# Moving two GpSimd residual additions ahead of the mixing weights, and one convolution tap behind the first scores

## The chip, the core and the metric

The kernel runs on one core of one Trainium2 chip. The metric is the device time of one execution in microseconds; the time before is the median of three runs. The profile is of a separate execution.

## What is computed

One transformer-like convolution layer over x of shape (128, 384, 14, 14), N = 196 pixels, 8 heads, key depth 32, value depth 128:

```
g  = groupnorm(x, 32 groups)
q, k, v4 = 1x1 convolutions of g (256, 256, 1024 channels), scaled and shifted
vl = depthwise 3x3 convolution of v4, scaled and shifted
attn = q k^T * scale + bias;  attn = th1w attn + th1b (mix over heads)
attn = softmax(attn);         attn = th2w attn + th2b (mix over heads)
o = relu(attn v + vl)
out = x + 1x1 convolution of o to 384 channels
```

## The kernel before

The 128 images are taken two at a time: 64 steps `t`, the first and the last written out and the 62 between them in a hardware loop. The work of each engine is an order written by hand; engines meet through semaphores, and what an engine has in its program runs strictly in that order.

In one step **TensorE** runs: 12 tiles of q, k and v (line 289 into `psA`), projection tiles 0 and 1 of the step before, 14 logit groups `n` (line 289 into `psL` and `psM`, two query rows of pixels each), projection tile 2, 14 mixing groups (line 396), and 8 groups of attention times value, `u` = 0 to 7 (line 418). Group u = 2 writes the bank that u = 0 used, so it waits until VectorE has added u = 0 into `acc` (semaphore `s_add`).

**VectorE** runs per step 64 taps of the depthwise convolution (line 687, `convs`), 16 low halves `q_lo` (709), two transposes (717), 28 scores (742, two for each logit group; each is an instruction that adds the bias and takes the maximum, and a short read of the accumulator), two reciprocals (752, 757), and then 8 additions (778) and 8 low halves `o_lo` (771). The taps come from one list: channel pair by channel pair, 16 taps each, and `convs(count)` takes the next `count`. Tap 0 of a channel reads `vpad` and `acc`, both in SBUF (shown as `psC<-vpad,par,shared`); taps 1 to 6 read `vpad` and PSUM (`psC<-vpad,par,psC`); tap 7 writes `acc` (`shared<-vpad,par,psC`). Whatever is left of the 64 runs behind the second reciprocal, in `convs(64)`, ahead of the first addition.

**GpSimd** (POOL) runs per step: two `k_lo` (841), four small instructions and the normalisation of the next pair (804), the mixing weights of image 0 and of image 1 (826, four instructions each: 448, 448, 448 and 224 columns), the three residual additions (815, `residual(t, m)`, one for each projection tile), and `x_lo` (809). Mixing weights of image 0 wait for the first reciprocal, those of image 1 for the second; a residual addition waits for ScalarE's eviction of its projection tile and, the first of them, for the loaded x (`s_res`). The names `acc` and `res` are parts of `shared`.

**SyncE** stores the result when all three residual additions are done, waits for that store, and then loads the next `res`.

Of the kernel before, what the change touches and what calls it, by code (L numbers as in the profile page):

```python
# [12 lines left out]
CT = DIM // P  # L13
# [30 lines left out]
def build(nc, A, out):  # L44
# [4 lines left out]
    with ExitStack() as ctx:  # L49
# [9 lines left out]
        def sem(name):  # L59
            return ctx.enter_context(nc.semaphore(name))  # L60
# [91 lines left out]
        s_x, s_res = sem("s_x"), sem("s_res")  # L152
# [54 lines left out]
        def wait_alone(eng, semaphore, value):  # L207

            eng.wait_ge(semaphore, value)
            eng.nop(nofuse=True)  # L210
# [400 lines left out]
        def _(dve):  # L611
# [78 lines left out]
            def step(t, first, last):  # L690
                todo = iter([(c, n) for c in range(0, VT, 2) for n in range(16)])

                def convs(count):
                    for _ in range(count):
                        nxt = next(todo, None)
                        if nxt:
                            conv(t, first, *nxt)

                if not first:
                    dve.wait_ge(s_olo, 8 * t)  # L700
                    dve.wait_ge(s_av_mm, 8 * t)
                low_half = iter([(kt, g) for kt in range(QT) for g in range(NH)])

                def mixed_low(count):
                    for _ in range(count):
                        kt, g = next(low_half)
                        dve.wait_ge(s_qhi, 16 * t + 8 * kt + g + 1)
                        dst, src = mixed(kt, g)
                        nc.vector.scalar_tensor_tensor(q_lo[dst], src, th1[:, kt, g:g + 1], q_hi[dst].bitcast(f32),  # L709
                                                       MUL, SUB).then_inc(s_qlo, 1)  # L710

                def turn(half):
                    c0 = half * (VT // 2)
                    dve.wait_ge(s_v_sb, VT * t + c0 + VT // 2)
                    src = vpad[:, c0:c0 + VT // 2, PITCH + 1:PITCH + 1 + 2 * PITCH * PITCH].rearrange(
                        "p c (i n) -> p c i n", i=2)[:, :, :, 0:BLOCKS * BLK]
                    nc.vector.transpose(turned[:, :, :, c0:c0 + VT // 2, :].rearrange("p i b c n -> p c (i b) n"),  # L717
                                        src).then_inc(s_turned, 1)

                if first:  # L720
                    dve.wait_ge(s_bias, 1)
                    dve.wait_ge(s_ones, 1)
                convs(6)
                for _ in range(8):
                    mixed_low(1)
                    convs(1)
                if not first:
                    dve.wait_ge(s_mix_mm, 14 * t)
                turn(0)
                convs(2)  # L730
                mixed_low(3)
                turn(1)
                mixed_low(5)
                convs(6)
                for n in range(RES):
                    if n == TURNED_ROW // 2:
                        dve.wait_ge(s_vt_out, OUTS * (t + 1))
                    wait_alone(dve, s_logit_mm, 14 * t + n + 1)
                    for r in (2 * n, 2 * n + 1):
                        img, b = divmod(r, RES)  # L740
                        at_ = (RES - 1 - b) * RES
                        nc.vector.tensor_tensor_reduce(  # L742
                            out=keys(img, b),
                            in0=logit_bank(n)[:, (r % 2) * PIX:(r % 2 + 1) * PIX].rearrange("p (r w) -> p r w", w=RES),
                            in1=bias[:, at_:at_ + PIX].rearrange("p (r w) -> p r w", w=RES),
                            scale=-1.0, scalar=3.4028234e38, op0=ADD, op1=ALU.min,
                            accum_out=nmax[:, img, b:b + 1]).then_inc(s_score, 1)
                    if n == 10:
                        dve.wait_ge(s_exp, 28 * t + 14)
                        if not first:  # L750
                            dve.wait_ge(s_mixw, 8 * t)
                        nc.vector.reciprocal(rinv[:, 0, :], rowsum[:, 0, :]).then_inc(s_rinv, 1)  # L752
                    if n:
                        convs(1)
                convs(3)
                dve.wait_ge(s_exp, 28 * t + 28)
                nc.vector.reciprocal(rinv[:, 1, :], rowsum[:, 1, :]).then_inc(s_rinv, 1)
                convs(3)
                convs(64)

                if first:
                    dve.wait_ge(s_wplo, 1)
                else:
                    dve.wait_ge(s_proj_mm, 3 * t)

                def low(u):
                    img, n = divmod(u, 4)
                    dve.wait_ge(s_relu, 8 * t + u + 1)
                    a = acc[:, 2 * n:2 * n + 2, img * IMG:img * IMG + PIX]
                    sl = (slice(None), slice(2 * n, 2 * n + 2), slice(img * PIX, (img + 1) * PIX))  # L770
                    nc.vector.scalar_tensor_tensor(o_lo[sl], a, 0.0, o_hi[sl].bitcast(f32), ALU.max, SUB).then_inc(s_olo, 1)

                for u in range(8):
                    img, n = divmod(u, 4)
                    dve.wait_ge(s_conv, 64 * t + 16 * (n + 1))
                    dve.wait_ge(s_av_mm, 8 * t + u + 1)
                    a = acc[:, 2 * n:2 * n + 2, img * IMG:img * IMG + PIX]
                    nc.vector.tensor_tensor(a, psA[:, n % 2, 0:COLS].rearrange("p (c n) -> p c n", c=2), a,  # L778
                                            ADD).then_inc(s_add, 1)
                    if u:  # L780
                        low(u - 1)
                low(7)
# [4 lines left out]
        def _(pool):  # L787
# [13 lines left out]
            def normalise(p):  # L801
                wait_alone(pool, s_rstd, p + 1)
                for i in range(2):
                    nc.gpsimd.tensor_scalar(xs[:, i, :, :], xs[:, i, :, :], gs[:, i, 0:1], rstd[:, i:i + 1],
                                            SUB, MUL).then_inc(s_xn, 1)
# [6 lines left out]
            def residual(t, m):  # L812

                wait_alone(pool, s_pout, 3 * (t - 1) + m + 1)
                nc.gpsimd.tensor_tensor(res[:, :, m, :], proj[:, m, :].rearrange("p (i n) -> p i n", i=2),
                                        res[:, :, m, :], ADD).then_inc(s_out, 1)

            def mixing_weights(t, first, img):

                if not first:  # L820
                    pool.wait_ge(s_mix_mm, 14 * (t - 1) + 7 * (img + 1))
                pool.wait_ge(s_rinv, 2 * t + img + 1)
                for b0 in range(0, RES, 4):
                    nb = min(4, RES - b0)
                    k2 = kron2[:, :, :].rearrange("p g i -> p (g i)").unsqueeze(1).broadcast_to([HP, nb, HP])
                    nc.gpsimd.tensor_tensor(mixw[0:HP, img, b0:b0 + nb, :], k2,  # L826
                                            rinv[:, img, b0:b0 + nb].unsqueeze(2).broadcast_to([HP, nb, HP]),
                                            MUL).then_inc(s_mixw, 1)
# [9 lines left out]
            def step(t, first, last):  # L838
                for kt in range(QT):
                    wait_alone(pool, s_khi, 2 * t + kt + 1)  # L840
                    nc.gpsimd.tensor_tensor(k_lo[:, kt, :], k[:, kt, :], k_hi[:, kt, :].bitcast(f32),  # L841
                                            SUB).then_inc(s_klo, 1)
                if not last:
                    reciprocal_deviation(t + 1)
                    normalise(t + 1)
                mixing_weights(t, first, 0)
                mixing_weights(t, first, 1)
                if first:
                    pool.wait_ge(s_wphi, 1)
                    nc.gpsimd.tensor_tensor(wp_lo[:, :, :], stage_p, wp_hi[:, :, :].bitcast(f32), SUB).then_inc(s_wplo, 1)  # L850
                if not first:
                    pool.wait_ge(s_res, 16 * t)
                    for m in range(CT):
                        residual(t, m)
                if not last:
                    pool.wait_ge(s_v_mm, VT * (t + 1))
                    if not first:
                        pool.wait_ge(s_out, 3 * t)
                    x_low(t + 1)
# [54 lines left out]
```

## Time and profile before

| | |
|---|---|
| median of 3 runs | 4620.49 us (4615.77 to 4624.45) |
| profiled execution, its own time | 4580.5 us |
| its span | 4578.4 us |
| PE busy | 4526.2 us (99%) |
| DVE busy | 4213.5 us (92%) |
| ACT busy | 3571.4 us (78%) |
| POOL busy | 1437.7 us (31%) |

The profiled execution is 39.99 us shorter than the median of the timed runs. Matmul records overlap one another, so a busy PE says only that something was under way. "Chain" below is the chain of work that ended last. A row of a timeline gives start, length, engine, line, operation, output<-inputs and shapes; the idle time ahead of it stands in brackets with what ended it. A record is longer than the step from it to the next one by about 0.1 us where instructions follow each other directly.

### The profile page before, as it was taken

How to read it: one execution, taken by the hardware profiler on the slowest of the kernel's cores; microseconds unless marked ns; L12 is line 12 of the kernel's file. 1: busy time of each engine (PE TensorE's matmuls, PEld its weight loads, DVE VectorE, ACT ScalarE, POOL GpSimd, SP SyncE). 2: the span in 40 equal slices, each digit the busy share in tenths (PEclk: the TensorE clock that was granted, in tenths of full speed). 3: DMA queues.
4: the chain of work that ended last, by engine and by line, in shares of the span. 5: the costliest groups of instructions: out<-in, count | busy, mean ns of one | idle time of the engine just before them, and what ended most of it. 6: DMA issues, size and time to landing. Idle time of an engine off the chain costs nothing.

```text
span 4578.4 us, 108323 instructions
## 1 busy us (share of the span) xinstructions
PE 4526.2 (99%) x33666; PEld 4504.7 (98%) x33666; DVE 4213.5 (92%) x10012; ACT 3571.4 (78%) x8508; POOL 1437.7 (31%) x1285
## 2 busy tenths in 40 slices
PE   6999999999999999999999999999999999999999
PEld 6999999999999999999999999999999999999999
DVE  8999999999999999999999999999999999999998
ACT  5877878778787787787877877878778777787786
POOL 3323233233332332323323323233233332332322
PEclk8999999999999999999999999999999999999999
DMA  3223222222232222322222223222222232222322
GB/s 91 77 67 96 64 80 81 75 84 67 77 96 64 80 80 69 91 64 80 86 74 80 76 68 96 64 80 85 73 82 69 75 96 64 80 80 71 89 64 75
DMA packets 210732, 356.04 MB, mean 78 GB/s; under 512 B 15842, under 2 KB 132690, under 8 KB 210644
## 3 DMA queue, kind: packets, MB, share of 16 engines
q1 hardware_dynamic: 210708, 355.74, 26.7%
q8 instruction: 13, 0.21, 0.0%
q14 instruction: 11, 0.09, 0.0%
HBM read 199.70 MB, written 155.98 MB: 78 GB/s over the span
## 4 chain that ended last, share of the span: by engine, by line
PE 95%; DVE 4%; issue 1%; DMA 0%; DVEq 0%; ACT 0%; POOL 0%; POOLq 0%
PE psA L289 44%; PE psA L418 13%; PE psL L289 13%; PE psM L289 10%; PE psM L396 8%; PE psL L396 6%; DVE psC L687 1%; DVE shared L687 1%; DVE shared L778 1%; DVE probs L742 0%; PE psA L302 0%; DVE xs L664 0%; DVE q_lo L709 0%; DMA xs<-in_x 0%; DVE probs L717 0%
## 5 line engine op out<-in xcount | busy, mean ns | idle before, releaser
L687 DVE SCALAR_TENSOR_TENSOR psC<-vpad,par,psC 128x406 f32<-128x406 f32 x3072 | 1804.4, 641 | 0.0
L576 ACT ACTIVATE probs<-probs,nmax 112x196 f32<-112x196 f32 x1792 | 803.1, 450 | 120.8 <-DVE nmax L742 112.6
L289 PE MATMUL psA<-x_hi,w_lo 128*128 128x392 f32 x2304 | 794.6, 345 | 15.5 <-DVE x_lo L668 15.5
L289 PE MATMUL psA<-x_hi,w_hi 128*128 128x392 f32 x2304 | 785.9, 341 | 0.0
L289 PE MATMUL psA<-x_lo,w_hi 128*128 128x392 f32 x2304 | 784.9, 341 | 0.0
L418 PE MATMUL psA<-qa,shared 105*128 105x196 f32 x4096 | 710.1, 332 | 16.2 <-DVE shared L778 8.2
L418 PEld LDWEIGHTS psA<-qa,shared 105*128 105x128 f32 x4096 | 677.7, 191 | 35.3 <-DVE shared L778 35.2
L841 POOL TENSOR_TENSOR k_lo<-qk,k_hi 128x392 fp32r<-128x392 f32 x128 | 160.1, 1250 | 1669.3 <-ACT k_hi L482 1669.3
L709 DVE SCALAR_TENSOR_TENSOR q_lo<-qk,th,q_hi 128x392 fp32r<-128x392 f32 x1024 | 618.8, 633 | 0.0
L453 ACT ACTIVATE o_hi<-shared 128x392 fp32r<-128x392 f32 x512 | 271.7, 531 | 426.4 <-DVE shared L778 426.3
L478 ACT ACTIVATE q_hi<-qk,th 128x392 fp32r<-128x392 f32 x1024 | 594.8, 618 | 2.1
L826 POOL TENSOR_TENSOR mixw<-kron,rinv 112x448 f32<-112x448 f32 (+1 forms) x512 | 462.4, 934 | 268.8 <-DVE rinv L752 156.2
L289 PE MATMUL psL<-k_hi,q_lo 128*112 128x196 f32 x2048 | 534.2, 261 | 6.6 <-DVE q_lo L709 6.6
L289 PE MATMUL psL<-k_lo,q_hi 128*112 128x196 f32 x2048 | 536.2, 262 | 0.0
L289 PE MATMUL psL<-k_hi,q_hi 128*112 128x196 f32 x2048 | 535.9, 262 | 0.0
L289 PE MATMUL psA<-o_hi,wp_lo 128*128 128x392 f32 x1536 | 526.5, 343 | 0.0
L289 PE MATMUL psA<-o_lo,wp_hi 128*128 128x392 f32 x1536 | 523.0, 341 | 0.0
L289 PE MATMUL psA<-o_hi,wp_hi 128*128 128x392 f32 x1536 | 521.0, 339 | 0.0
L687 DVE SCALAR_TENSOR_TENSOR psC<-vpad,par,shared 128x406 f32<-128x406 f32 x512 | 331.9, 671 | 142.8 <-ACT shared L448 142.7
L502 ACT ACTIVATE vpad<-psA,par 128x392 f32<-128x392 f32 x512 | 349.6, 683 | 144.8 <-PE psA L289 138.2
L289 PEld LDWEIGHTS psA<-x_hi,w_lo 128*128 128x128 f32 x2304 | 434.3, 188 | 15.9 <-issue 15.9
L396 PE MATMUL psM<-mixw,probs 113*105 113x112 f32 x4096 | 436.0, 260 | 0.0
(83 smaller groups left out, 10804.0 us busy)
## 6 DMA issues: line engine op xcount, KB each, us to landing
by_key<-probs SPq DMA_DIRECT2D x512, 224.0 KB, 3.6
qa<-by_key SPq DMA_DIRECT2D x128, 448.0 KB, 4.3
qk<-by_key SPq DMA_DIRECT2D x128, 448.0 KB, 7.0
xs<-in_x SPq DMA_DIRECT2D x64, 588.0 KB, 5.1
shared<-in_x SPq DMA_DIRECT2D x64, 588.0 KB, 3.8
out<-shared SPq DMA_DIRECT2D x63, 588.0 KB, 3.0
qa<-in_wqkv SPq DMA_DIRECT2D x3, 768.0 KB, 8.1
stage_wp<-in_wp SPq DMA_DIRECT2D x1, 1536.0 KB, 10.5
```

Source lines behind the costliest of these rows:

```text
L289: last = nc.tensor.matmul(dst, w, r, start=(begin and n == 0), stop=(end and n == 2))
L396: mm = nc.tensor.matmul(bank[:, jc, :, b, :], probs[0:HP + 1, img, 2 * n + b, jc * HALF:(jc + 1) * HALF], mixw[0:HP + 1, img, 2 * n + b, : ...
L418: mm = nc.tensor.matmul(psA[:, u % 2, e * PIX:(e + 1) * PIX], vt[0:HALF, img, jc, g * D:(g + 1) * D], attn[:, img, jc, g, :], start=(jc == ...
L453: nc.scalar.activation(o_hi[:, 2 * n:2 * n + 2, img * PIX:(img + 1) * PIX], acc[:, 2 * n:2 * n + 2, img * IMG:img * IMG + PIX], ACT.Relu). ...
L478: nc.scalar.activation(q_hi[dst], src, ACT.Copy, scale=th1[:, kt, g:g + 1]).then_inc(s_qhi, 1)
L502: nc.scalar.activation(dst[:, :, 0:RES, 0:RES], psA[:, m % 2, 0:COLS].rearrange("p (i r w) -> p i r w", i=2, w=RES), ACT.Identity, bias=qk ...
L576: nc.scalar.activation(row, row, ACT.Exp, bias=nmax[:, img, b:b + 1], scale=-1.0, accum_out=rowsum[:, img, b:b + 1]).then_inc(s_exp, 1)
L687: nc.vector.scalar_tensor_tensor(a if tap == 7 else sums, src, taps[:, c, TAPS[tap]:TAPS[tap] + 1], a if tap == 0 else sums, MUL, ADD).the ...
L709: nc.vector.scalar_tensor_tensor(q_lo[dst], src, th1[:, kt, g:g + 1], q_hi[dst].bitcast(f32), MUL, SUB).then_inc(s_qlo, 1)
L778: nc.vector.tensor_tensor(a, psA[:, n % 2, 0:COLS].rearrange("p (c n) -> p c n", c=2), a, ADD).then_inc(s_add, 1)
L826: nc.gpsimd.tensor_tensor(mixw[0:HP, img, b0:b0 + nb, :], k2, rinv[:, img, b0:b0 + nb].unsqueeze(2).broadcast_to([HP, nb, HP]), MUL).then_ ...
L841: nc.gpsimd.tensor_tensor(k_lo[:, kt, :], k[:, kt, :], k_hi[:, kt, :].bitcast(f32), SUB).then_inc(s_klo, 1)
```

## The change

On VectorE, the logit loop takes one tap behind the scores of group n = 0 too; so far it took one behind each of n = 1 to 13. On GpSimd, the residual additions of projection tiles 0 and 1 (with the wait for `s_res`) go ahead of the mixing weights; tile 2 stays behind them.

```diff
@@ VectorE, in the loop over the 14 logit groups
                         nc.vector.reciprocal(rinv[:, 0, :], rowsum[:, 0, :]).then_inc(s_rinv, 1)
-                    if n:
-                        convs(1)
+                    convs(1)
                 convs(3)
@@ GpSimd, in step
                     reciprocal_deviation(t + 1)
                     normalise(t + 1)
+                if not first:
+                    pool.wait_ge(s_res, 16 * t)
+                    residual(t, 0)
+                    residual(t, 1)
                 mixing_weights(t, first, 0)
                 mixing_weights(t, first, 1)
...
                 if not first:
-                    pool.wait_ge(s_res, 16 * t)
-                    for m in range(CT):
-                        residual(t, m)
+                    residual(t, 2)
```

VectorE's order at the first scores, before: two logit groups are scored in a row, then the first tap follows.

```order
50 L742 ISA probs,nmax<-psL,bias 112x14x14
51 L742 ISA nmax 112x1
52 L742 ISA probs,nmax<-psL,bias 112x14x14
53 L742 ISA nmax 112x1
54 L742 ISA probs,nmax<-psL,bias 112x14x14
55 L742 ISA nmax 112x1
56 L687 SCALAR_TENSOR_TENSOR psC<-vpad,par,psC 128x406
```

The same place now:

```order
50 L742 ISA probs,nmax<-psL,bias 112x14x14
51 L742 ISA nmax 112x1
52 L687 SCALAR_TENSOR_TENSOR psC<-vpad,par,psC 128x406
53 L742 ISA probs,nmax<-psL,bias 112x14x14
54 L742 ISA nmax 112x1
55 L742 ISA probs,nmax<-psL,bias 112x14x14
56 L742 ISA nmax 112x1
57 L687 SCALAR_TENSOR_TENSOR psC<-vpad,par,psC 128x406
```

A tap stands ahead of the scores of group 1. VectorE's order from the first reciprocal on, groups 10 to 12, before:

```order
101 L752 RECIPROCAL rinv<-rowsum 112x14
102 L687 SCALAR_TENSOR_TENSOR shared<-vpad,par,psC 128x406
103 L742 ISA probs,nmax<-psM,bias 112x14x14
104 L742 ISA nmax 112x1
105 L742 ISA probs,nmax<-psM,bias 112x14x14
106 L742 ISA nmax 112x1
107 L687 SCALAR_TENSOR_TENSOR psC<-vpad,par,shared 128x406
108 L742 ISA probs,nmax<-psL,bias 112x14x14
```

and now:

```order
102 L752 RECIPROCAL rinv<-rowsum 112x14
103 L687 SCALAR_TENSOR_TENSOR psC<-vpad,par,shared 128x406
104 L742 ISA probs,nmax<-psM,bias 112x14x14
105 L742 ISA nmax 112x1
106 L742 ISA probs,nmax<-psM,bias 112x14x14
107 L742 ISA nmax 112x1
108 L687 SCALAR_TENSOR_TENSOR psC<-vpad,par,shared 128x406
109 L742 ISA probs,nmax<-psL,bias 112x14x14
```

Every tap stands one group sooner: the two taps 0, with both inputs in SBUF, stand behind the scores of groups 10 and 11 instead of 11 and 12. GpSimd's order in the loop, as the difference:

```order
+L814 TENSOR_TENSOR shared<-proj,shared 128x2x196
+L820 ISA
+L825 TENSOR_TENSOR mixw<-kron,rinv 112x448 x3
+L825 TENSOR_TENSOR mixw<-kron,rinv 112x224
+L820 REGISTER_ALU
+L825 TENSOR_TENSOR mixw<-kron,rinv 112x448 x3
+L825 TENSOR_TENSOR mixw<-kron,rinv 112x224
 L209 REGISTER_ALU
-L815 TENSOR_TENSOR shared<-proj,shared 128x2x196
-L856 ISA
-L858 REGISTER_ALU
-L809 TENSOR_TENSOR x_lo<-xs,x_hi 128x1176
+L814 TENSOR_TENSOR shared<-proj,shared 128x2x196
```

Two residual additions come ahead of the eight mixing-weight instructions, and one is left behind them.

## Rows read from the trace of the kernel before

**Rows 1.** The page's chain that ended last, by engine

```profile
PE 95%; DVE 4%; issue 1%; DMA 0%; DVEq 0%; ACT 0%; POOL 0%; POOLq 0%
```

**Rows 2.** Chain in order of time, one step: start, length, what

```profile
2008.41 8.23 PE psA L418 x48
...
2046.84 1.18 PE psM L289 x12
...
2065.53 1.54 PE psM L396 x16
...
2076.27 1.36 PE psA L418 x8
...
2077.90 0.64 DVE shared L687
...
2079.07 8.23 PE psA L418 x48
```

**Rows 3.** Timeline of VectorE behind the last scores

```profile
2061.94 2.28 DVE L687 SCALAR_TENSOR_TENSOR psC<-vpad,par,psC 128x406 f32<-128x406 f32 x4
2064.13 0.23 DVE L757 RECIPROCAL rinv<-rowsum 112x14 f32<-112x14 f32 x1
```

**Rows 4.** Timeline of VectorE at the first scores

```profile
2046.38 0.08 DVE L742 DVE_READ_ACCUMULATOR2_ANT nmax<- 112x1 f32 x1
2046.99 0.36 DVE L742 CUSTOM_DVE_ANT_0 probs<-psL,bias 112x196 f32<-112x196 f32 x1 [0.53 <-PE psL L289]
```

**Rows 5.** Waits of the whole span: total, times, longest

```profile
DVE probs L742 <- PE psL L289: 34.4, 64, 1.2
```

**Rows 6.** Timeline of VectorE, second step

```profile
140.28 0.64 DVE L687 SCALAR_TENSOR_TENSOR psC<-vpad,par,psC 128x406 f32<-128x406 f32 x1
140.82 0.36 DVE L742 CUSTOM_DVE_ANT_0 probs<-psM,bias 112x196 f32<-112x196 f32 x1
```

**Rows 7.** Timeline of VectorE, logit groups 10 to 12

```profile
2058.55 0.56 DVE L687 SCALAR_TENSOR_TENSOR shared<-vpad,par,psC 128x406 f32<-128x406 f32 x1
2059.02 0.36 DVE L742 CUSTOM_DVE_ANT_0 probs<-psM,bias 112x196 f32<-112x196 f32 x1
...
2059.58 0.65 DVE L687 SCALAR_TENSOR_TENSOR psC<-vpad,par,shared 128x406 f32<-128x406 f32 x1
2060.19 0.37 DVE L742 CUSTOM_DVE_ANT_0 probs<-psL,bias 112x196 f32<-112x196 f32 x1
...
2060.76 0.70 DVE L687 SCALAR_TENSOR_TENSOR psC<-vpad,par,shared 128x406 f32<-128x406 f32 x1
```

**Rows 8.** Timeline of GpSimd, same step (rows may overlap)

```profile
2052.06 4.66 POOL L804 TENSOR_SCALAR xs<-xs,gs,rstd 128x588 f32<-128x588 f32 x2 [0.18 <-POOL rstd L799]
2058.78 0.93 POOL L826 TENSOR_TENSOR mixw<-kron,rinv 112x448 f32<-112x448 f32 x1 [2.07 <-DVE rinv L752]
2059.68 1.34 POOL L826 TENSOR_TENSOR mixw<-kron,rinv 112x448 f32<-112x448 f32 x1
...
2067.71 1.02 POOL L815 TENSOR_TENSOR shared<-proj,shared 128x392 f32<-128x392 f32 x1
2067.71 4.05 POOL L815 TENSOR_TENSOR shared<-proj,shared 128x392 f32<-128x392 f32 x3
```

**Rows 9.** Timelines of GpSimd and VectorE, first step

```profile
69.08 1.83 POOL L826 TENSOR_TENSOR mixw<-kron,rinv 112x448 f32<-112x448 f32 x2 [2.66 <-DVE rinv L752]
69.95 1.41 DVE L687 SCALAR_TENSOR_TENSOR psC<-vpad,par,shared 128x406 f32<-128x406 f32 x1
...
78.76 6.71 POOL L850 TENSOR_TENSOR wp_lo<-stage_wp,wp_hi 128x3072 fp32r<-128x3072 f32 x1
80.80 5.12 DVE L687 SCALAR_TENSOR_TENSOR psC<-vpad,par,shared 128x406 f32<-128x406 f32 x1
```

**Rows 10.** Timeline: channel 6's tap 0, third step and a middle step

```profile
231.53 1.46 DVE L687 SCALAR_TENSOR_TENSOR psC<-vpad,par,shared 128x406 f32<-128x406 f32 x1
...
2069.68 0.65 DVE L687 SCALAR_TENSOR_TENSOR psC<-vpad,par,shared 128x406 f32<-128x406 f32 x1
```

## The prediction

> **What bounds the kernel now.** I read first the page's chain that ended last: 95% of it is PE, 4% is DVE [rows 1]. So nearly all of the time is matmuls that this change does not touch, and what it can give or take lies in the 4%. Then the chain in order of time, for one step in the middle [rows 2]. Attention times value, groups u = 0 and 1, starts at 2076.27 and takes 1.36 us, to 2077.63. Group 2 starts only at 2079.07: a stall of 1.44 us, and inside it the chain runs over VectorE (its last tap at 2077.90, then the addition of u = 0). The same place one step earlier is 2008.41, so a step takes 70.66 us and the stall is 2.0% of it. I see no other wait of PE in a step of the loop. Last, VectorE's timeline behind the last scores: from 2061.94 taps run without a gap, broken only by the second reciprocal [rows 3], to the last tap at 2077.90. TensorE thus waits for a VectorE that has 30 taps to do there. A tap taken out of this run shortens the stall by one tap, as long as 1.44 us are not used up and the tap finds a free place elsewhere.
>
> **The change, the tap.** A tap in a run costs (2064.13 - 2061.94) / 4 = 0.55 us [rows 3]. Its new place is behind group 0's scores. There VectorE issues its last accumulator read at 2046.38 and starts the next score at 2046.99, with 0.53 us of idle time that TensorE ends [rows 4]; this wait comes 64 times, 34.4 us in all, once a step [rows 5]. From a tap's start to the start of a score behind it takes 0.54 us where the score's data are ready [rows 6]. So the score of group 1 could start at 2046.38 + 0.54 = 2046.92, and the data allow 2046.99: the tap is hidden, at no cost. If that cover were short by 0.1 us, the later groups would absorb it: two scores and a tap are 2 x 0.285 + 0.55 = 1.12 us, against 1.18 us that TensorE takes for a group [rows 2], 0.06 us a group. Here 0.285 is half of 2059.58 - 2059.02, rounded up [rows 7].
>
> **The change, the taps behind groups 10 and 11.** Each later tap of the loop stands one group sooner, so the two taps 0 (both inputs in SBUF) meet other instructions of GpSimd. This is the only place where I find a cost. In the first step such a tap stood 5.12 us while GpSimd worked on `wp_lo`, from 78.76 to 85.47, and ended at 85.92, 0.45 us behind it; another took 1.41 instead of 0.65 us and ended at 71.36, 0.45 us behind the mixing weights that ran to 70.91 [rows 9]. The other way round, the mixing weights that began at 2059.68, behind a tap 0 that ended at 2060.23, took 1.34 instead of 0.93 us and ended at 2061.02, 0.79 us behind the tap [rows 7, 8]. The two engines exclude one another there, and I take these two figures, 0.45 and 0.79, as the rule of the sum. Taps that read PSUM show no such thing.
>
> GpSimd's new timetable: the normalisation ends at 2056.72; two residual additions of 1.02 us, records overlapping by 0.04, end at about 2058.68 [rows 8]. Their inputs are old by then (tiles 0 and 1 are evicted before the logits, `res` is loaded in the step before). The mixing weights of image 0 wait for the reciprocal and started at 2058.78 anyway. The additions fit into 2.07 us in which GpSimd was idle [rows 8].
>
> The tap behind group 10 starts at 2058.55. Behind the addition it can end at 2058.68 + 0.45 = 2059.13 at the earliest, and by itself it ends between 2059.11 (0.56, as what stands there now) and 2059.20 (0.65): no delay [rows 7]. The first mixing weights are now behind this tap and end 0.79 later, 2059.90 to 2059.99. The tap behind group 11, begun at 2059.58, then ends 0.45 behind that, 2060.35 to 2060.44, where it ended at 2060.23. A score starts 0.10 before the record of the tap ahead of it ends [rows 6], so group 12's starts at 2060.25 to 2060.34 instead of 2060.19: 0.06 to 0.15 late. Group 13 gives 0.06 of it back. Taps behind the last scores start 0 to 0.09 us late; I take 0.04.
>
> **The change, GpSimd's rest.** Mixing weights of image 0 finish near 2062.7 as before (the fourth, shorter one starts late but the third meets no tap 0 now); the first mixing matmul starts at 2065.53 [rows 2], 2.8 us later, and that is the cover. Tile 2's addition runs 2067.71 to 2068.73 where three ran to 2071.76 [rows 8]. The store's descriptors on SyncE and the reload of `res` behind it move 3 us forward; the next load of x stays, since it waits for `x_lo`. Nobody on the chain waits for these. One small gain: the third addition used to start with channel 6's tap 0. In the third step the tap lost and took 1.46, in a middle step 0.65 us [rows 10]; so in two steps, the third and the last, the stall was 0.81 us longer. With one addition, over at 2068.73, the tap at 2069.13 meets none.
>
> **The sum.** Gain of a step: 0.55 - 0.04 = 0.51 us. It comes in 63 steps; in the first, `wp_lo` holds up the same tap 0 to the same time, and nothing is won. 63 x 0.51 = 32.1, and 2 x 0.81 = 1.6: 33.7 us. The profiled execution takes 4580.5 (span 4578.4 and 2.1 around it) and would take 4546.8. The median of the timed runs lies 40.0 us above it; I take the saving off that as it is: 4620.5 - 33.7 = 4586.8, say **4587 us**. Bounds: with no late taps 0.55 a step, 36.3 us, 4584; if the additions start 0.1 late, behind their waits, both delays grow by 0.1 and the step gains 0.41, 27.4 us, 4593. With the spread of the runs before, +-4 us, the likeliest case lies within 4580 to 4597.
>
> **A rule weighed.** The rows say that a waiting tap ends 0.45 us behind GpSimd's record, so that it starts in effect 0.2 us before that record is over; and the tap at 2059.58 was not delayed at all, 0.13 us before the first mixing weights ended at 2059.71 [rows 7, 8]. The Trainium skill (SBUF — State Buffer, section "SBUF: two separate sides") says that a VectorE operation with two SBUF inputs and a GpSimd operation that reads SBUF exclude one another, that whoever starts first keeps the ports for the whole instruction, and that the other fully blocks. The exclusion agrees with the trace; "whole instruction" to the record's end does not, by these 0.2 us. By that rule taken to the letter the step would gain about nothing (first rival), by the rows 0.51 us.
>
> **Rivals.** (1) *The block eats the gain.* If a tap 0 starts only at the end of GpSimd's record, the tap behind group 10 ends at 2058.68 + 0.65 = 2059.33, the mixing weights at 2060.26, the tap behind group 11 at 2060.91, and group 12 starts 0.62 late; less 0.06, that is 0.56 against 0.55. The time stays at about 4620. For it: the residual addition ends only 0.13 us behind the tap's start, so little is to spare. Against it: the three cases in rows 7 to 9.
>
> (2) *The tap behind group 11 loses to two mixing-weight instructions: slower.* In the first step the tap at 69.95 waited for an instruction that had not begun: GpSimd's second, which ended at 70.91 and so began at 69.98. If that happens each step, the second mixing weights end at 2059.95 + 0.89 = 2060.84, the tap at 2061.29, group 12 starts at 2061.19, 1.0 late, less 0.06: 0.94 - 0.55 = 0.39 us lost a step, 24.6 us, less 1.6: 4643. It decides when the tap's start is nearer than some 0.03 us to the start of GpSimd's next instruction. Here the tap begins at 2059.58 and the next would begin at 2059.86 or later, 0.28 us apart; 0.10 us were enough in the loop (2059.58 against 2059.68) [rows 7, 8].
>
> (3) *No change in the stall*, since the second reciprocal waits for something else, or the score of group 1 slips: 4619. ScalarE's exponentials end well ahead of that reciprocal and TensorE looks back three groups for a score, so I give it little.
>
> **Chances.** Likeliest 0.78; rival 1 0.12 (with part of the gain or none); rival 2 0.07; rival 3 0.03. The range of 4579 to 4608 takes in the likeliest case and the half of rival 1 in which a third or more of the gain is left. About 0.2% (9 us) can be told from no change: faster 0.82, same 0.10, slower 0.08.
>
> **What would show it.** The step in the chain: 70.15 us instead of 70.66, and PE's stall ahead of group u = 2 at 0.93 instead of 1.44. VectorE's wait ahead of group 1's score gone, and that score no later against the logits. First mixing weights about 1.2 us long (blocked), the tap behind group 11 0.8 to 0.85 us, group 12's score 0.06 to 0.15 late. The third addition always 1.02. I am wrong if a tap 0 takes 1.2 us or more, if the two additions start late, or if the stall shrinks and another wait of PE appears.

## The result, and the profile after

| | before | after |
|---|---|---|
| median of the timed runs | 4619.75 us (4615.77 to 4624.45, 4 runs) | 4552.59 us (4551.43 to 4554.10, 4 runs) |
| ratio | | 0.9858 (95% interval 0.9843 to 0.9874) |
| profiled execution | 4580.5 us | 4552.6 us |
| PE busy | 4526.2 us | 4507.4 us |

The change made the kernel 67.2 us faster. The direction was forecast, the size was not: 33.7 us were forecast, and the measured time lies below the range. The two profiled executions differ by only 27.9 us. So there are two questions: why the profiles differ by what they do, and where the other 39 us are. Before the change the profiled execution was 39 us shorter than the timed ones; now it is one of the four timed runs (4552.60), and these lie within 2.7 us of one another.

The page's chain by engine, after, against [rows 1]:

```profile
PE 98%; DVE 1%; issue 0%; DMA 0%; ACT 0%; POOL 0%; POOLq 0%; DVEq 0%
```

The chain in order of time, the attention-times-value stretches of three steps in a row (start, length, what), against [rows 2]:

```profile
1993.37 10.63 PE psA L418 x64
...
2063.63 10.63 PE psA L418 x64
...
2133.90 10.63 PE psA L418 x64
```

A step is 70.26 us long instead of 70.66, and the 64 matmuls of this stretch are one piece of 10.63 us, with no wait in it. Before, the same 64 stood from 2076.27 to 2079.07 + 8.23 = 2087.30, 11.03 us. TensorE lost 0.40 us a step there and now loses nothing. That answers most of the first question: 63 x 0.40 = 25.2 us, and the two late taps of the first profile are 2 x 0.81 = 1.6, together 26.8 of the 27.9. About 1 us more lies ahead of the second step's stretch, which begins at 167.30 us before and at 166.27 after; in e8, the kernel before once more, it begins at 166.58, so most of that differs between executions of one program.

VectorE's timeline after, from the first reciprocal to group 13, against [rows 7]:

```profile
2045.76 0.24 DVE L752 RECIPROCAL rinv<-rowsum 112x14 f32<-112x14 f32 x1
2045.91 0.58 DVE L687 SCALAR_TENSOR_TENSOR psC<-vpad,par,shared 128x406 f32<-128x406 f32 x1
2046.41 0.35 DVE L742 CUSTOM_DVE_ANT_0 probs<-psM,bias 112x196 f32<-112x196 f32 x1
...
2046.97 0.75 DVE L687 SCALAR_TENSOR_TENSOR psC<-vpad,par,shared 128x406 f32<-128x406 f32 x1
2047.64 0.35 DVE L742 CUSTOM_DVE_ANT_0 probs<-psL,bias 112x196 f32<-112x196 f32 x1
...
2048.75 0.35 DVE L742 CUSTOM_DVE_ANT_0 probs<-psL,bias 112x196 f32<-112x196 f32 x1
```

GpSimd's in the same step, against [rows 8]:

```profile
2044.03 2.02 POOL L814 TENSOR_TENSOR shared<-proj,shared 128x392 f32<-128x392 f32 x2
2046.14 3.78 POOL L825 TENSOR_TENSOR mixw<-kron,rinv 112x448 f32<-112x448 f32 x4
...
2055.08 1.03 POOL L814 TENSOR_TENSOR shared<-proj,shared 128x392 f32<-128x392 f32 x1
```

The tap behind group 10 is not held up (0.58). The one behind group 11 is, by about 0.1 us (0.75), and group 12's score stands 1.73 us behind the start of the tap of group 10, where it stood 1.64 behind. The two additions fit into GpSimd's idle time.

VectorE's timeline after, the end of the taps and the first two additions of attention times value:

```profile
2064.20 1.17 DVE L687 SCALAR_TENSOR_TENSOR shared<-vpad,par,psC 128x406 f32<-128x406 f32 x2
2065.29 0.55 DVE L777 TENSOR_TENSOR shared<-psA,shared 128x392 f32<-128x392 f32 x1
2066.41 0.57 DVE L777 TENSOR_TENSOR shared<-psA,shared 128x392 f32<-128x392 f32 x1 [0.56 <-PE psA L418]
```

The addition of u = 0 starts 1.66 us behind the beginning of TensorE's stretch in the chain (2065.29 - 2063.63). Before, it was 2.18 (2078.45 - 2076.27 [rows 2]); its row on the timeline of before is this one:

```profile
2078.45 1.16 DVE L778 TENSOR_TENSOR shared<-psA,shared 128x392 f32<-128x392 f32 x2
```

So VectorE's run ends 0.52 us sooner, and 0.51 was forecast. Now VectorE waits 0.56 us for u = 1 there, and not TensorE for VectorE.

### The profile page after: what moved, and what is told of

Read it like the earlier page. It is cut to its first block, busy times and chain, and to the rows that moved or that the text cites. A ratio compares the mean times of both kernels' runs of the same rounds, so it can differ in the third digit from the quotient of the medians.

```text
span 4550.6 us, 108323 instructions
## 1 busy us (share of the span) xinstructions
PE 4507.4 (99%) x33666; PEld 4505.0 (99%) x33666; DVE 4204.0 (92%) x10012; ACT 3569.6 (78%) x8508; POOL 1361.2 (30%) x1285
## 4 chain that ended last, share of the span: by engine, by line
PE 98%; DVE 1%; issue 0%; DMA 0%; ACT 0%; POOL 0%; POOLq 0%; DVEq 0%
PE psA L289 45%; PE psA L418 15%; PE psL L289 13%; PE psM L289 10%; PE psM L396 8%; PE psL L396 6%; DVE psC L687 1%; PE psA L302 0%; DVE q_lo L709 0%; DVE w_lo L657 0%; DVE xs L664 0%; DVE probs L742 0%; DMA xs<-in_x 0%; DVE probs L717 0%; DVE shared L687 0%
## 5 line engine op out<-in xcount | busy, mean ns | idle before, releaser
L418 PE MATMUL psA<-qa,shared 105*128 105x196 f32 x4096 | 693.7, 330 | 7.5 <-DVE shared L777 7.5
L825 POOL TENSOR_TENSOR mixw<-kron,rinv 112x448 f32<-112x448 f32 (+1 forms) x512 | 449.0, 907 | 146.4 <-DVE rinv L756 125.4
```

The source lines that it names most:

```text
L418: mm = nc.tensor.matmul(psA[:, u % 2, e * PIX:(e + 1) * PIX], vt[0:HALF, img, jc, g * D:(g + 1) * D], attn[:, img, jc, g, :], start=(jc == ...
```

## The experiments

Two theories of the missing 39 us. **Race:** GpSimd's addition for projection tile 2 and VectorE's tap 0 of channel 6 begin almost together, and each can hold up the other; in the timed executions of before, the addition came first in most steps and cost VectorE 0.81 us each time, where in the profiled one it did so in two. **Offset:** the timed executions were longer for another reason, and the tap brought all of it. And two sizes for the stall at group u = 2: 1.44 us (the prediction's) or 0.40.

The record numbers the chips of the runs below 0 (e1 to e4), 5 (e5 to e7) and 1 (e8), and does not name that of the first comparison. The kernel before took 4628.8 to 4629.2 us there in the median, where it took 4619.75 in the first comparison. Ratios below are against the kernel before on the same chip; steps lost to the addition are counted against 4579, the time without any. The first comparison's own profile gives the same base: 4580.5 less two losses of 0.81 is 4578.9.

### e1: only the residual additions moved

```diff
@@ from the changed kernel: VectorE's loop as before
-                    convs(1)
+                    if n:
+                        convs(1)
```

> Theory R (race): in the timed runs of before, tile 2's residual addition and channel 6's tap 0 start within some 0.01 us of each other and VectorE loses 0.81 us in most steps, where it lost in two in the profiled execution; (4619.75 - 4580.5) / 0.81 = 48 further steps. Moving two residual additions away ends the race and nothing else: profiled and timed both about 4579, which is 41 us less than before timed and 1.6 less than before profiled. Rival O (offset): the timed executions of before are 39 us longer for another reason, and what the changed kernel gained beyond its profile came with the tap: timed 4615 to 4620, profiled 4579. Rival T (the tap gains all): as O.

Measured: 4579.02 us (4577.54 to 4579.29), ratio 0.9891 (0.9874 to 0.9907); the profiled execution is one of these four runs, 4579.29. The race forecast 4579, the offset theory 4615 to 4620. The step is still 70.67 us long, with the stall in it:

```profile
PEld psA L418 <- DVE shared L778: 33.7, 64, 6.4
```

This is the wait of TensorE's weight loads for VectorE's addition over the whole span (total, times, longest). Without the longest, which is the first step's, it is 27.3 us in 63 steps, 0.43 each. The move of the two additions is worth 41 us by itself against the first comparison's 4619.75, and 50 against the 4628.78 of this chip. The tap is worth the rest: 4579.02 - 4552.59 = 26.4 us, 0.42 a step; step by step the two traces differ by 0.40 us.

### e2: only the tap moved

```diff
@@ from the kernel before: VectorE
-                    if n:
-                        convs(1)
+                    convs(1)
```

> The tap moved, the three residual additions together as before. Channel 6's tap 0 now starts 0.55 us sooner, inside the second residual addition, waits for it and ends 0.45 us behind its record: about 0.38 us late, so VectorE's run ends 0.55 - 0.38 = 0.17 us sooner. Theory R: no near tie any more (the tap is waiting long before the third addition), steps of 70.50, timed and profiled both about 4580.5 - 63 x 0.17 - 1.6 = 4568. If the tap then loses to the third addition too, it ends 1.4 us late and the step grows by 0.85: 4630. Rival T: 4552 as the changed kernel. Rival O: 4608 timed, 4568 profiled.

Measured: 4615.4 us (4614.47 to 4616.62), ratio 0.9971 (0.996 to 0.9983); profiled within that. None of the numbers given (4552, 4568, 4608 or 4630). Timelines of VectorE and GpSimd in one step:

```profile
2084.16 2.34 DVE L687 SCALAR_TENSOR_TENSOR psC<-vpad,par,shared 128x406 f32<-128x406 f32 x2
...
2084.69 1.36 POOL L814 TENSOR_TENSOR shared<-proj,shared 128x392 f32<-128x392 f32 x1
```

In the kernel before, the two taps 0 of channels 6 and 7 took 1.20 us together and the addition waited:

```profile
2069.68 1.20 DVE L687 SCALAR_TENSOR_TENSOR psC<-vpad,par,shared 128x406 f32<-128x406 f32 x2
```

Now they take 2.34. The first waits for the second addition, as forecast (1.02 to 1.03 us in each step). But then the third addition came in between the two taps: it took 1.36 us, so it waited for the first tap, and the second tap waited for it (1.40 us). I had assumed that a waiting addition lets both taps through, as it does in that row. The step is 71.27 us long, 0.60 more than without any loss. The rows add up to that: the two taps lose 1.03 + 1.40 - 2 x 0.64 = 1.15 us, and the moved tap takes 0.55 out of the run. So the tap alone brings 0.3% here (13.4 us) and the additions alone 49.8; together they bring some 76 (4628.8 against the 4552.6 of the first comparison's changed kernel), more than their sum: the tap moved a tap 0 into the additions that the other part takes away.

### e3: a small memset more on GpSimd

```diff
@@ from the kernel before: GpSimd, pad is a spare tile
                     for m in range(CT):
+                        if m == 2:
+                            nc.gpsimd.memset(pad[:, 0:1], 0.0)
                         residual(t, m)
```

> The kernel before with one small GpSimd memset (about 0.1 us, of a spare tile) ahead of tile 2's residual addition, so that the addition starts 0.05 to 0.1 us later than channel 6's tap 0. It adds work. Theory R: VectorE wins in every step, timed and profiled both about 4579, 41 us less than before timed. Rivals O and T: timed 4620.

Measured: 4578.17 us (4578.01 to 4578.33), ratio 0.989 (0.9873 to 0.9906). The kernel does more than before and takes 51 us less. GpSimd's timeline, and VectorE's tap:

```profile
2068.01 0.10 POOL L856 MEMSET pad<- 128x1 f32 x1
2068.07 2.05 POOL L816 TENSOR_TENSOR shared<-proj,shared 128x392 f32<-128x392 f32 x1
```

```profile
2068.05 1.19 DVE L688 SCALAR_TENSOR_TENSOR psC<-vpad,par,shared 128x406 f32<-128x406 f32 x2
```

The addition starts 0.02 us behind the tap, and it is the addition that waits, 2.05 us instead of 1.02; the taps take 1.19 together. All 63 steps go this way. GpSimd's wait costs nothing, VectorE's does. This rules out the offset theory: nothing else of the kernel was changed, and the tap was not moved.

### e4: a small memset more on VectorE

```diff
@@ from the kernel before: VectorE, ahead of the last run of taps
+                nc.vector.memset(pad[:, :], 0.0)
                 convs(64)
```

> The kernel before with one small VectorE memset (128 columns of a spare tile, 0.1 to 0.2 us) ahead of the last run of taps, so that the addition starts first in every step. Theory R: VectorE loses in every step, 0.81 us each, and the memset's net 0.05 to 0.15 us lies on the chain: 4580.5 + 61 x 0.81 + 63 x 0.1 = 4636, profiled and timed alike (4633 to 4640). Rivals O and T: profiled 4587, timed 4627.

Measured: 4628.69 us (4627.59 to 4629.64), ratio 0.9999 (0.999 to 1.0009). The tap loses in all 63 steps, 1.34 us instead of 0.65. VectorE's two taps and GpSimd's three additions in one step:

```profile
2090.99 1.89 DVE L688 SCALAR_TENSOR_TENSOR psC<-vpad,par,shared 128x406 f32<-128x406 f32 x2
...
2088.91 2.98 POOL L817 TENSOR_TENSOR shared<-proj,shared 128x392 f32<-128x392 f32 x3
```

My sum was 7 us too high. It added the memset's 0.11 us to a loss of 0.81, but a tap that comes 0.11 us later waits 0.11 less for the same addition; the end of the wait is GpSimd's. So the run doesn't show what the memset costs. It equals the kernel before, since that one loses here in every step too (e8). The timed runs alone would not tell the theories apart (4627 was the rivals' forecast); the profiled execution does, at 4629.41 against their 4587.

### e8: the kernel before, profiled once more

> The kernel before, unchanged, profiled once more. Theory R: the profiled execution's time is 4579 plus 0.81 for each step in which channel 6's tap 0 takes 1.46 instead of 0.65 us, and the steps with the long tap are 71.48 long: with the timed runs' 4628.8, 61 or 62 such steps if the profiled execution falls like the timed ones, 2 of them if it falls as the first profile (4580.5). If a profiled execution takes 4620 or more with short taps 0 in most steps, the theory is wrong.

Measured: 4629.23 us (4627.86 to 4630.30), the profiled execution at the same length (span 4627.2). VectorE's and GpSimd's timelines in one step:

```profile
2090.09 2.00 DVE L687 SCALAR_TENSOR_TENSOR psC<-vpad,par,shared 128x406 f32<-128x406 f32 x2
```

```profile
2088.11 2.98 POOL L815 TENSOR_TENSOR shared<-proj,shared 128x392 f32<-128x392 f32 x3
```

and two pieces of its chain, one step apart:

```profile
2100.29 8.23 PE psA L418 x48
...
2171.76 8.23 PE psA L418 x48
```

This is the same program as in [rows 2] and [rows 8], and it is another kernel in its time. The two taps take 2.00 us together, the three additions 2.98 instead of 4.05, and the step is 71.47 us long instead of 70.66. Channel 6's tap 0 is the long one in all 63 steps (61 or 62 were forecast for this case), against two of 63 in the first profile. 61 more losses at 0.81 us are 49.4 us, and the spans differ by 4627.2 - 4578.4 = 48.8.

### e5: two taps cut short

```diff
@@ from e1: VectorE, conv()
+                few = 1 if (c0, n) in ((6, 6), (6, 7)) else ACC_ROWS
+                src = src[:, 0:few, :]
...
+                a, sums = a[:, 0:few, :], sums[:, 0:few, :]
```

> The two residual additions moved as in e1, no tap moved, but two taps of channels 6 and 7 (tap 3) cut from 406 columns to 14: this leaves most of these two taps out. VectorE's last run is about 0.9 us shorter. Theory S (the stall ahead of group u = 2 is the gap between two matmuls there, 2078.61 to 2079.07 less 0.17, and 0.10 of slow restart: 0.40 us a step): the gain stops at 0.40, 4579.0 - 63 x 0.40 = 4554, steps of 70.27. Theory P (the prediction's: a stall of 1.44): 4579.0 - 63 x 0.9 = 4522.

Measured: 4552.82 us (4551.73 to 4553.96), ratio 0.9836 (0.9819 to 0.9852). The kernel leaves out 28 of the 29 rows of these two taps. VectorE's last tap then ends 0.82 us sooner against TensorE's first matmul (1.61 us behind its start, in the median step, where it was 2.43 in e1), and this brought 26.2 us, 0.42 a step: no more than the 26.4 that the moved tap's 0.52 us brought. Only 0.40 us were there to win, not 1.44. The chain shows the same unbroken piece as the changed kernel's:

```profile
2063.30 10.63 PE psA L418 x64
```

### e6 and e7: how much cover is left

```diff
@@ from the changed kernel: VectorE, ahead of the last run of taps (e6: one of 128 columns)
+                for j in range(3):
+                    nc.vector.memset(pad[:, j, :], 0.0)
                 convs(64)
```

> The changed kernel with one VectorE memset of 128 columns ahead of the last run of taps, net 0.11 us as in e4. Theory S: VectorE's run shrank by 0.52 us and the step by 0.40, so 0.12 us of cover is left and the memset just fits: 4552 to 4555. Theory P: every 0.11 us shows, 4559.5.

> The changed kernel with three VectorE memsets of 104 columns there, net 0.4 to 0.5 us. Theory S: 0.12 of it is covered, the rest shows: 4552.6 + 63 x (0.3 to 0.4) = 4571 to 4578. Theory P: 4578 to 4584. If TensorE did not wait for VectorE at this place at all: 4553.

Measured: e6 4552.23 us (4551.48 to 4553.25), ratio 0.9834 (0.9818 to 0.9851); e7 4563.31 us (4562.93 to 4563.81), ratio 0.9858 (0.9841 to 0.9874). One memset is free, as forecast from the stall of 0.40. Three are not, but they cost less than either theory gave (4571 or more): 10.7 us, 0.17 a step. I had taken them for 0.4 to 0.5 us together. Two pieces of e7's chain say 70.43 us a step, where the changed kernel's is 70.26:

```profile
2068.32 10.80 PE psA L419 x64
...
2138.75 10.80 PE psA L419 x64
```

The three memsets shift VectorE's addition by 0.31 us. The rows of e7, the first matmul and the addition of u = 0:

```profile
2068.16 3.33 PE L419 MATMUL psA<-qa,shared 105*128 105x196 f32 x18
...
2070.29 0.55 DVE L780 TENSOR_TENSOR shared<-psA,shared 128x392 f32<-128x392 f32 x1
```

The addition stands 2.13 us behind the start of the first matmul's record, where it is 1.82 in the changed kernel (2065.29 - 2063.47; this record starts 0.16 us ahead of the chain's piece). So 0.31 - 0.17 = 0.14 us are covered; 0.12 was forecast.

## Why the prediction was right or wrong

**Right, with its size: the tap.** It fits behind group 0 (the next score stands 0.61 us behind it, where 0.54 was the least). **Right: the exclusion at groups 10 and 11.** The tap behind group 10 was not delayed, the one behind group 11 took 0.75 us (forecast 0.8 to 0.85), group 12's score came 0.09 late (0.06 to 0.15). The rule "0.45 us behind GpSimd's record, 0.79 behind the tap" held: 0.45 and 0.78 in a middle step of the changed kernel. **Right: the shift of VectorE's run**, 0.52 against 0.51. Rivals 1 and 2 did not occur, neither in the profile nor, by the agreement with it, in the timed runs.

**Wrong, one term of the sum: "a stall of 1.44 us".** The chain's row ends with group u = 0 at 2077.63 and the next PE row begins with group 2. What lies between is not all stall: group u = 1's eight matmuls run in it, and the chain doesn't show them, since there it follows VectorE. The count says it: 8 and 48 of the 64 matmuls [rows 2]. The stall is 11.03 - 10.63 = 0.40 us (e1, e5). Of the tap's 0.51 us only 0.40 could show: 63 x 0.51 = 32.1 us should have been 63 x 0.40 = 25.2, and 26.4 were measured (e1 against the changed kernel). "PE's stall at 0.93 instead of 1.44" was wrong with it; it is nothing instead of 0.40. The rest of the tap's time is the 0.12 to 0.14 us of cover in e6 and e7.

**Wrong, the larger term: "2 x 0.81 = 1.6" and "I take the saving off that as it is".** The mechanism was in the prediction: one addition instead of three ends a near tie that VectorE loses at 0.81 us a time, as in the third step [rows 10]. Its size was taken from one execution. The timed ones lost (4619.75 - 4579.02) / 0.81 = 50 times, not 2, and that is the 39 us by which they were longer than the profiled one. I had this difference in front of me, on the same page as the near tie, and passed it on as a constant. The additions' 40.7 us and the tap's 26.4 make up the 67.2 measured, but that is no test, since both are counted from e1's time. The tests are e1 and e3, where the losses are gone and the time is 4579 and 4578, and e8, where an execution of the kernel before loses in each of 63 steps and takes 48.8 us more. That the timed executions of the first comparison lost in about 50 steps is worked out from their times; no trace of one of them was kept.

**The rule weighed.** The Trainium skill (SBUF — State Buffer, section "SBUF: two separate sides") names the exclusion, and all runs agree with it. That the one who starts first keeps the ports, as the section also says, the shared access of the two engines to SBUF, is borne out where starts are far apart (e4, where the addition starts 0.12 us sooner and wins 63 times). In the near tie the start of the record does not decide: in the first profile the addition's record began 2 to 25 ns ahead of the tap's, and VectorE won 61 of 63; in e8 it began 14 to 21 ns ahead, and VectorE lost 63 of 63. In 22 steps that VectorE won, the addition was ahead by the same 14 to 21 ns. These starts do not show what tips it, and no run here settles it.

What stays open is why one execution of the same program falls one way and another the other, and whether that belongs to the chip or to the moment. On the three chips of the experiments every timed run of the kernel before took 4625 to 4631 us, which is some 57 steps lost or more; the first comparison's took 4616 to 4624.

## What to carry to other kernels

Where timed and profiled executions of one program differ by more than their spread, ask what near tie in the profile could fall the other way, and price it times the number of steps. Where two engines hold one another up, let them meet with a distance between their starts: here one memset of 0.10 us more on the engine that has time was worth 51 us. A gap between two rows of one engine in the chain need not be idle time (here 1.44 us of gap held 0.40 us of stall); count the instructions, or look at that engine's own waits, before a saving is sized by it.

## What the hardware showed that I had not expected

The same program has steps of 70.66 or 71.47 us at the same granted clock (0.997 and 0.998), and in both profiled executions it stayed with one of them in at least 61 of 63 steps. By their times, the runs of 4616 to 4624 us were mixtures; no trace shows one. Whether an engine keeps the shared access between two instructions of its own is not fixed: in e2 GpSimd's addition came in between two taps that follow each other directly, while in e3 the two taps went through one behind the other (1.19 us) and the addition waited 2.05. No run here shows what decides between the two.
